# A gathered step as one part: one ReLU over six tiles in place of two over three

## What is computed

```python
def _gine_layer(x, src, dst, edge_attr, eps, We, be, W1, b1, gamma, beta, W2, b2):
    e = edge_attr @ We + be
    m = jax.nn.relu(x[src] + e)
    agg = jax.ops.segment_sum(m, dst, num_segments=x.shape[0])
    h = ((1.0 + eps) * x + agg) @ W1 + b1
    mu = jnp.mean(h, axis=0)
    var = jnp.mean(jnp.square(h - mu), axis=0)
    h = (h - mu) * jax.lax.rsqrt(var + BN_EPS) * gamma + beta
    h = jax.nn.relu(h)
    return jax.nn.relu(h @ W2 + b2)
```

## Time and profile before

| | |
|---|---|
| median of 3 runs | 1668.04 us (1665.87 to 1668.96) |
| the profiled execution | 1669.31 us |
| its span, first to last instruction | 1667.6 us |
| mean granted TensorE clock | 0.943 |
| PE matmul busy | 1427.5 us (86%) |
| VectorE busy | 1183.6 us (71%) |
| GpSimd busy | 1027.5 us (62%) |
| ScalarE busy | 955.8 us (57%) |
| DMA | 343.20 MB, mean 206 GB/s |
| chain that ended last | PE 43%, POOL 16%, DVE 14%, issue 11%, DMA 8%, ACT 7% |

### The profile page before, as it was taken

How to read it: one execution, slowest core, us unless ns; L and a number is a source line. 1 busy time by engine, 2 the same in 40 slices (tenths; PEclk the granted TensorE clock), 3 DMA queues, 4 the chain that set the end, 5 groups by cost and what they waited for, 6 DMA issues and landing times.

```text
span 1667.6 us, 21159 instructions
## 1 busy us (share of the span) xinstructions
PE 1427.5 (86%) x6662; PEld 600.8 (36%) x6734; DVE 1183.6 (71%) x2391; ACT 955.8 (57%) x1211; POOL 1027.5 (62%) x1070
## 2 busy tenths in 40 slices
PE   2777988879898988988889998897989989898597
PEld 2233333335443432333433332234433323334264
DVE  7679788886666887767476876776667777675644
ACT  3545454543457766766467776674677767673221
POOL 2777777777326777777066777773367777760133
PEclk9797999978999999999899999999999999999799
DMA  8666777787357777777267887784578787867443
GB/s 264 201 195 192 209 211 206 209 260 213 107 152 242 223 225 218 227 223 211 68 204 236 235 235 226 223 249 122 156 236 229 235 234 225 254 200 259 167 150 102
DMA packets 119091, 343.20 MB, mean 206 GB/s; under 512 B 20712, under 2 KB 24892, under 8 KB 118718
## 3 DMA queue, kind: packets, MB, share of 16 engines
q0 software_dynamic: 85248, 278.41, 57.2%
q1 hardware_dynamic: 32318, 60.78, 11.4%
q10 hardware_dynamic: 1408, 2.56, 0.5%
HBM read 323.61 MB, written 19.96 MB: 206 GB/s over the span
## 4 chain that ended last, share of the span: by engine, by line
PE 43%; POOL 16%; DVE 14%; issue 11%; DMA 8%; ACT 7%; DVEq 1%; POOLq 0%; SPq 0%; ACTq 0%
PE ps L1944 40%; POOL ring L899 15%; DVE ring L1110 8%; DMA ring<-x_table,idxT 6%; ACT ring L1707 5%; DVEq L1141 1%; ACT aggT L1771 1%; PE ps L2021 1%; DVE aggT L1150 1%; DMA ring<-in_x 1%; DMA zT<-slot_table 1%; PE ps L2113 1%; PE ps L2432 0%; DVE ring L1459 0%; DVE ring L1023 0%
## 5 line engine op out<-in xcount | busy, mean ns | idle before, releaser
L899 POOL DMA_INDIRECT ring<-x_table,idxT x1014 | 985.5, 972 | 472.7 <-issue 295.4
L1110 DVE SCALAR_TENSOR_TENSOR ring<-ps,wT,ring 128x512 f32<-128x512 f32 x930 | 626.9, 742 | 143.8 <-DMA ring<-x_table,idxT 139.3
L1707 ACT ACTIVATE ring<-ring 128x1536 f32<-128x1536 f32 x322 | 470.7, 1480 | 265.5 <-DVE ring L1110 264.7
L1944 PE MATMUL ps<-ring,onehot 128*32 128x512 f32 x2028 | 378.0, 638 | 133.4 <-ACT ring L1707 121.1
L1944 PE MATMUL ps<-zT,xT 128*32 128x512 f32 (+2 forms) x752 | 285.8, 605 | 0.0
L1944 PE MATMUL ps<-ring,zT 128*128 128x512 bf16 x1014 | 260.2, 382 | 9.2 <-issue 4.0
L1747 ACT ACTIVATE zT<-ps 128x512 f32<-128x512 f32 x336 | 193.2, 595 | 114.6 <-PE ps L1944 106.4
L1944 PEld LDWEIGHTS ps<-ring,onehot 128*32 128x32 f32 x2028 | 59.2, 110 | 336.6 <-ACT ring L1707 277.8
L1944 PE MATMUL ps<-w,zT 128*125 128x512 f32 (+2 forms) x320 | 147.1, 623 | 15.1 <-ACT zT L1855 15.1
L1944 PEld LDWEIGHTS ps<-ring,zT 128*128 128x128 bf16 x1080 | 93.0, 98 | 185.4 <-ACT zT L1747 77.4
L1944 PE MATMUL ps<-aggT,w 128*128 128x256 f32 (+2 forms) x512 | 150.3, 443 | 6.0 <-DVE aggT L1150 6.0
(11 more groups left out here) (331 smaller groups left out, 1365.7 us busy)
## 6 DMA issues: line engine op xcount, KB each, us to landing
ring<-x_table,idxT POOLq DMA_INDIRECT x1014, 3.7
zT<-slot_table SPq DMA_DIRECT2D x36, 312.5 KB
w<-in_L_gnn_W SPq DMA_DIRECT2D x8, 1024.0 KB, 11.1
ring<-in_L_ffn_W SPq DMA_DIRECT2D x16, 512.0 KB, 9.7
x_table<-ring SPq DMA_DIRECT2D x24, 250.0 KB
x_table<-ring SPq DMA_DIRECT2D x9, 256.0 KB
stage<-in_x ACTq DMA_DIRECT2D x9, 256.0 KB
pair_table<-mix SPq DMA_DIRECT2D x9, 256.0 KB
```

The costliest lines, as they stand in the source:

```text
L899: gp.indirect_dma_start(out=to, out_offset=None, in_=table[:, :], in_offset=bass.IndirectOffsetOnAxis(ap=idx, axis=0)).then_inc(done, 16)
L1110: ins = v.scalar_tensor_tensor(out=at[:, x, :], in0=terms[:, :], scalar=wT[:, c, u:u + 1], in1=at[:, x, :], op0=ALU.mult, op1=ALU.add)
L1707: a.activation(at, at, ACT.Relu).then_inc(relu_done, 1)
L1944: return nc.tensor.matmul(o, lhsT, rhs, start=start, stop=stop)
```

## The change

`parts_of` now returns one part for every step but step 0. `summed`, `relu_done` and the number of ReLUs follow from it in the same functions: one semaphore increment by VectorE behind all six adds, one ReLU of 128 x 3072 elements on ScalarE, one wait on TensorE ahead of six sums. In `group_sums`, only the place that stands ahead of the part is left in front, and the others stand behind the six sums.

```diff
@@ -107,11 +107,10 @@
     def early_at(e):
         return min(j for j, es in EARLY_MIXED.items() if e in es)
 
-    FIRST_PART = U // 2
 
     def parts_of(l, j):
 
-        return [range(1)] if j == 0 else [range(FIRST_PART), range(FIRST_PART, U)]
+        return [range(1)] if j == 0 else [range(U)]
 
 
 
```

## The result

The changed kernel takes **1733.33 us** (median of 4 runs, 1727.21 to 1738.1), beside 1667.49 us for the kernel before on the same chip: ratio 1.0393, interval 1.0355 to 1.0431. That is 66 us more where 20 were forecast, and far outside the range of 1673 to 1703. The profiled execution took 1730.72 us, its span is 1729.0 us.

The account below looks back on a forecast made before the run. The prediction took GpSimd's gathers, 7.5 us a step, to set the pace for most of a layer. Mixed-layer starts 6.9, ends 6.4 and layer 0 6.9 made +20.2 us on 1668.04: 1688.2 us, range 1673 to 1703.

Parts of the forecast that it names:

- Steps 1 to 41 hide it in the 11.8 us.: Layer 0: GpSimd needs the sums 11.8 us after they end, so later sums cost nothing in these steps.
- Case B: Step with VectorE just in time: ReLU +1.29 us, two more rounds of sums +0.86, together +2.15 us.
- Start of a mixed layer: Layers 1 to 3, up to step 3's sums: three ReLUs in series, 2.3 us later per layer, 6.9 in all.
- case A: Step with ScalarE behind and both halves ready: +0.78 us until TensorE is free.
- Steps 4 to 16 of a mixed layer: TensorE takes 22.3 us for three steps, just below GpSimd's 22.5, so GpSimd isn't held up: 0 us.
- End of a mixed layer: Layers 1 to 3, last whole step 37: nothing behind hides the delay, 2.15 us each, 6.4 in all.
- Steps 42 to 50 of layer 0: TensorE's long run: step 42 costs 2.15 us, steps 43 and 44 nothing, 45 to 50 4.8, together 6.9.
- Hidden: Rival: slack of four slots hides the longer step everywhere, also at starts and ends; 1668 us, chance 0.12.
- Faster: Rival: ScalarE paces the mixed layers and its ReLU falls from 2.85 to 2.77 us; 1662 us, chance 0.06.
- TensorE takes over from GpSimd: Rival: steps 4 to 16 of layers 2 and 3 fall behind; +8 us, 1696 or more, chance 0.15.
- Places in program order: Rival: mixed layers' places wait behind the sums, 0.86 us more each; +22 us, 1710, chance 0.05.

Follow-up runs that it names:

- e3: Kernel before, with one part only in steps 19 to 42 of layer 0, halves elsewhere: 1701.81 us, ratio 1.02.
- e5: Kernel before, halves kept, but in layer 0 TensorE waits for both halves' ReLUs before its first sum: 1685.3 us, ratio 1.012.
- e6: Kernel before, halves kept, but in layer 0 ScalarE starts the first half's ReLU only after all six adds: 1685.85 us, ratio 1.0127.
- e12: Changed kernel plus two unread matmuls ahead of TensorE's wait for the ReLU in steps 1 to 3 of the mixed layers: 1731.32 us, 1.0379 to the kernel before.
- e2: Kernel before, with one part only in layers 1 to 3, halves in layer 0: 1686.97 us, ratio 1.0126.
- e4: Kernel before, with one part only in steps 1 to 18 and 43 to 50 of layer 0: 1680.98 us, ratio 1.0079.
- e11: Changed kernel plus three unread matmuls ahead of TensorE's ReLU wait in odd steps 19 to 41 of layer 0: 1726.02 us, 1.0348 to the kernel before.
- e1: Kernel before, with one part only in layer 0, halves in layers 1 to 3: 1710.16 us, ratio 1.0258.

## Why the prediction was wrong, point by point

- **The step that failed: "Steps 1 to 41 hide it in the 11.8 us."** The 11.8 us were read at one place, the end of step 42, and taken as slack that a delay uses once. That is right only if the later step doesn't inherit the delay. Here it does, through the list product: the loop adds 3 us at each of its laps, and the slack lasts until step 25. Cost: 33 us in e3, forecast 0 but for step 42. The trace of before showed it, had I looked: VectorE's 22.1 us of waits for TensorE at line 1452, and a chain that ended last which ran through that line in steps 27 to 29. The step is wrong as a mechanism, not only in size.
- **Case B, +2.15 a step.** Right in its parts: ReLU 2.76 against 2.77, four rounds 1.91 us, and e5 and e6 show that the two halves of the sum (0.86 and 1.29) both count. (The second half began 0.03 us behind the sixth add by the earlier trace rows, not 0.06; the sum doesn't use it.) But the round of 0.43 us holds at the full clock only. At the lower level it is 0.83 to 0.86 (step 27), and there the case costs up to 1.7 us more.
- **Start of a mixed layer, 2.3 each.** In layer 3 exactly so. GpSimd's first gather of step 7, in layers 1, 2 and 3, to be held against the earlier trace rows:

```profile
584.20 0.95 POOL L898 DMA_INDIRECT ring<-x_table,idxT  x1 [6.42 <-issue]
```
```profile
945.69 0.94 POOL L898 DMA_INDIRECT ring<-x_table,idxT  x1 [6.12 <-PE ps L1943]
```
```profile
1303.18 0.94 POOL L898 DMA_INDIRECT ring<-x_table,idxT  x1 [6.11 <-PE ps L1943]
```

  In layer 1 the profile puts the wait down to issue, before and after, but the gather starts 1.1 us behind the sums of step 3 in both, as in the other layers it starts 0.8 us behind them. Layer 3's moved by 56.8, of which 54.5 had come before that layer's first ReLU. In layers 1 and 2 the start costs 5.6 us, of which 3.3 come with the slow sums of steps 1 and 2 (absent in e12). With one part in the mixed layers alone (e2) the same sums ran at the full clock and each ReLU moved by 0.77 us, as case A had it.
- **Steps 4 to 16 of a mixed layer, 0 for GpSimd.** Right. In layer 2 its first gather of step 7 is 50.8 us later than before and that of step 12 51.1 (932.87 in the earlier trace rows):

```profile
983.98 0.95 POOL L898 DMA_INDIRECT ring<-x_table,idxT  x1 [0.30 <-issue]
```

  The margin is right too. Between the sums of step 8 and those of step 11 TensorE now takes 22.5 us, where the sum had 22.3 and before 20.3:

```profile
980.07 0.63 PE L1943 MATMUL ps<-ring,onehot 128*32 128x512 f32 x3
...
1002.52 0.63 PE L1943 MATMUL ps<-ring,onehot 128*32 128x512 f32 x3
```

  Against before it falls back by 6 us between steps 7 and 18, but before it gained as much on GpSimd. So the slack neither grows nor runs out: 2.0 us behind step 8 (the sum had 1.6), 3.4 behind step 18.
- **End of a mixed layer, 2.15 each.** From the gather of step 37 to the last sum, layers 1, 2 and 3 lose 2.8, 4.0 and 3.1. The rest of layer 2's goes with a lower clock in the fine steps, 0.81 where before had 1.00. The same stretch in both:

```profile
1194.00:1203.00 9.00, 7.25 (x32) 4.10 (x27) 3.66 (x9) 4.38 (x5) 2.39 (x3) 0.81 0.42 117
```
```profile
1140.00:1149.00 9.00, 7.25 (x38) 4.15 (x38) 6.38 (x14) 5.53 (x6) 3.78 (x4) 1.00 0.59 168
```

  Starts and ends together lose 23.4 us, and the mixed layers only 18.3, mostly because between the last sum of a layer and the first ReLU of the next 2.8, 1.5 and 1.5 us come back, which the sum didn't foresee.
- **Steps 42 to 50 of layer 0, 6.9.** Not confirmed. The sums are 38.2 us late at step 41, 37.5 at step 43, 34.8 at step 44 and 41.2 at step 50, so these steps add 3.0 in all. Step 42's 2.15 doesn't show, step 44 gives back 2.7 that the sum didn't have, and steps 45 to 50 cost 6.4 where it had 4.8. In e4, which has halves up to step 42, steps 43 to 50 add 3.9.
- **The rivals.** "Hidden" and "Faster" are out. "TensorE takes over from GpSimd" has the right mechanism in the wrong layer: TensorE's chain took the lead in layer 0, where I hadn't looked, and not in the mixed layers. "Places in program order" is out too: 0.04 us behind the first round of sums a place starts, though nine more passes stand ahead of it in the program, and the list of the change put it behind all six tiles:

```profile
964.75 0.63 PE L1943 MATMUL ps<-ring,onehot 128*32 128x512 f32 x3 [0.85 <-ACT ring L1706]
964.79 0.62 PE L1943 MATMUL ps<-zT,xT 128*32 128x512 f32 x1
```

  By the rule of the Trainium skill (TensorE: Matmul & The Clock Gate, The mechanism) it would have started behind them; this case's rows differ from it, before and after.

## What to carry to other kernels

Slack between two engines is no stock until you know that nothing brings a delay round. Before costing a change at nothing, follow each product of the late engine to its reader and ask whether that reader stands ahead of the next step's input: then the delay returns every lap, and the lap, not the slack, has to be held against the pace. A sign of such a loop in the profile of before is a wait, however short, that runs against the direction of the pipeline, as VectorE's for TensorE did here. Joining instructions saved ScalarE 26.6 us here and cost 66 (e6 pays 19 without joining any). The Trainium skill (Perfetto Trace Analysis, Optimizing Scalar/DVE Operations) names both sides, a fixed overhead that grouping spares and, where ScalarE isn't saturated but leaves others idle, instructions broken up so that work is done sooner; this case's trace agrees with the second, with ScalarE busy for 54% of the span.

## What the hardware showed that I had not expected

Behind longer waits TensorE's next work was often slower. After idle times of 2.35 and 3.09 us twelve passes took 3.03 and 3.59 us instead of 1.91, at a granted clock of 0.63 and 0.54; with products of no use ahead of the same wait they took 1.92 and 1.91 (e12, e11). Over layer 0 the granted clock was 0.86 where before had 0.89. What brings the fall about isn't settled: in layer 3 and in e2 the same sums stood behind the same 2.35 us of idle and ran at the full clock, and in step 23 of layer 0 they did so behind 3.40 us, in the change and likewise in e1, e3 and e12. Here are step 23 and layer 3 of the change:

```profile
240.56 1.91 PE L1943 MATMUL ps<-ring,onehot 128*32 128x512 f32 x12 [3.40 <-ACT ring L1706]
...
1278.07 1.92 PE L1943 MATMUL ps<-ring,onehot 128*32 128x512 f32 x12 [2.35 <-ACT ring L1706]
```

So the idle time right ahead isn't all of it, and which earlier stretch makes the difference stays open.
